# Feed-forward of a post-norm transformer layer: 32-bit operands become pairs of 16-bit halves, the psum banks go in three pairs, and work moves from VectorE to ScalarE and GpSimd

## What is computed

```python
q, k, v = x @ Wq + bq, x @ Wk + bk, x @ Wv + bv      # 16 heads of 128, q scaled by 128 ** -0.5
q, k = rotary(q), rotary(k)
attn = softmax(causal(q @ k.T)) @ v                   # per batch and head
x1 = layernorm(x + attn @ Wo + bo)                    # no gain, no offset
gate = silu((x1 @ w_gate) * s_gate)                   # weights int8, one scale for each column
up = (x1 @ w_up) * s_up
out = layernorm(x1 + ((gate * up) @ w_down) * s_down)
```

## Time and profile before

| | |
|---|---|
| median of 3 runs | 1843.8 us (1839.7 to 1846.18) |
| the profiled execution, own time | 1839.86 us |
| its span in the trace | 1838.1 us |
| PE busy | 1661.6 us, 90% of the span |
| DVE, ACT, POOL busy | 1556.7 (85%), 1397.9 (76%), 1411.7 (77%) us |
| mean granted TensorE clock | 0.993 of full speed |

### The profile page before, as it was taken

How to read it: one execution, slowest core, us unless ns; L and a number is a source line. 1 busy time by engine, 2 the same in 40 slices (tenths; PEclk the granted TensorE clock), 3 DMA queues, 4 the chain that set the end, 5 groups by cost and what they waited for, 6 DMA issues and landing times. The chain is left out here.

```text
span 1838.1 us, 34107 instructions
## 1 busy us (share of the span) xinstructions
PE 1661.6 (90%) x10508; PEld 1062.2 (58%) x10508; DVE 1556.7 (85%) x3734; ACT 1397.9 (76%) x2514; POOL 1411.7 (77%) x1331
## 2 busy tenths in 40 slices
PE   5799898898999999999999999989999999889997
PEld 3355555454555555555555555555555555468886
DVE  7799999998888888888888888888888888867886
ACT  4688778778888888888888888788888888754443
POOL 4888888788878888888888887898888887724554
PEclk9899999999999999999999999999999999999999
DMA  3666767657666676667666666676676876640001
GB/s 115 135 125 134 138 150 136 137 98 153 133 126 124 125 142 123 118 132 145 127 123 125 135 137 124 117 148 125 117 124 120 171 144 122 105 104 13 24 24 35
DMA packets 645027, 218.43 MB, mean 119 GB/s; under 512 B 610544, under 2 KB 617200, under 8 KB 644720
## 3 DMA queue, kind: packets, MB, share of 16 engines
q1 hardware_dynamic: 620784, 174.30, 50.7%
q10 hardware_dynamic: 24064, 41.95, 8.1%
HBM read 48.40 MB, written 16.78 MB: 35 GB/s over the span
## 5 line engine op out<-in xcount | busy, mean ns | idle before, releaser
L1223 DVE SCALAR_TENSOR_TENSOR planes<-S,recip,planes 128x128 f16<-128x128 f32 (+7 forms) x512 | 417.3, 815 | 130.6 <-ACT planes L883 129.9
L883 ACT ACTIVATE planes<-S,recip 128x128 f16<-128x128 f32 (+7 forms) x512 | 378.7, 740 | 155.3 <-DVE recip L1284 140.2
L874 ACT ACTIVATE S<-p_row,neg_max 128x128 f32<-128x128 f32 (+7 forms) x512 | 381.1, 744 | 131.1 <-DVE neg_max L1213 130.1
L548 POOL TENSOR_TENSOR swap<-swap,sin_t 128x512 f32<-128x512 f32 x256 | 326.3, 1275 | 169.4 <-ACT swap L896 169.4
L1213 DVE CUSTOM_DVE_ANT_0 p_row<-S,mask_row,to_score 128x128 f32<-128x128 f32 (+7 forms) x512 | 416.9, 814 | 11.1 <-PE S L1533 8.9
L542 POOL TENSOR_TENSOR rot<-rot,swap 128x512 f32<-128x512 f32 x252 | 320.1, 1270 | 68.4 <-DVE rot L1273 64.1
L896 ACT ACTIVATE swap<-S,bqx 64x512 f32<-64x512 f32 x512 | 349.6, 683 | 21.1 <-PE S L1554 8.3
L1472 PE MATMUL O<-PT,VA 128*128 128x512 f16 (+3 forms) x1152 | 216.2, 329 | 58.3 <-issue 41.8
L1472 PE MATMUL O<-PT,VB 128*128 128x512 f16 (+3 forms) x1152 | 214.7, 327 | 58.8 <-issue 41.5
L1533 PE MATMUL S<-QKA 128*128 128x512 f16 (+4 forms) x1152 | 231.7, 329 | 5.6 <-DVE planes L1223 3.5
L1533 PE MATMUL S<-QKB 128*128 128x512 f16 (+4 forms) x1152 | 229.8, 327 | 4.9 <-POOL QKB L586 2.7
(11 more groups left out here) (209 smaller groups left out, 2724.0 us busy)
## 6 DMA issues: line engine op xcount, KB each, us to landing
PT<-planes SPq DMA_TRANSPOSE x512, 3.4
WA<-w_d ACTq DMA_DIRECT2D x24, 256.0 KB, 3.7
WB<-w_d ACTq DMA_DIRECT2D x24, 256.0 KB, 2.7
attn_d<-resid ACTq DMA_DIRECT2D x16, 256.0 KB, 2.6
x_raw<-in_x_cols SPq DMA_DIRECT2D x12, 256.0 KB, 3.7
WVA<-wv_d ACTq DMA_DIRECT2D x12, 256.0 KB, 2.7
resid<-in_x_rows ACTq DMA_DIRECT2D x12, 256.0 KB, 4.0
WVB<-wv_d ACTq DMA_DIRECT2D x12, 256.0 KB, 2.7
```

The costliest lines, as they stand in the source:

```text
L548: nc.gpsimd.tensor_tensor(swap[:, c, :], swap[:, c, :], sin_t[:, half], ALU.mult).then_inc(sin_done, 1)
L874: nc.scalar.activation(row_psum(n, s)[:, 0:cols], p_row[:, k % 2, 0:cols], ACT.Exp, bias=neg_max[:, s:s + 1], scale=-1.0, accum_out=row_su ...
L883: nc.scalar.activation(row_halves(n, s)[:, 0], row_psum(n, s)[:, 0:cols].rearrange("p (j q) -> p j q", q=P), ACT.Copy, scale=recip[:, s:s ...
L1223: nc.vector.scalar_tensor_tensor(halves_of[:, 1], row_psum(n, s)[:, 0:cols].rearrange("p (j q) -> p j q", q=P), recip[:, s:s + 1], halves_ ...
```

## The change

The feed-forward matmuls get float16 operands, in high and low halves for x and fuse, and plain float16 for the int8 weights. x is scaled by 2 to the 11th (X1_UP) and the up product by a factor f_up taken from the scales, both taken out again through s_gate, s_up and s_down; these factors are made in head 58 by a few small instructions (weigh_s, sum_s, take_s, scale_s). Groups 1 to 7 use three bank pairs in turn instead of two; there are eight fuse buffers for six, and four product and Silu buffers for two each; the down product comes three steps back. The bias sums move from VectorE to GpSimd, the normalising from VectorE to ScalarE (VectorE computes `shift` = -mean * rstd for it), and the conversion of all ffn weights to GpSimd, two pieces at the end of each of heads 58, 60 and 62.

The diff, cut to its core:

```diff
-    fuse = [at(AT_QK + 4096 * i, f"fuse{i}", [P, 2, GQ], F32R) for i in range(6)]
-    ffn_w = [at(AT_X + 8192 * i, f"ffn_w{i}", [P, KT * INTER], F32R)[:, :] for i in range(2)] + [
-        at(AT_QK + 24576, "ffn_w2", [P, JT * DIM], F32R)[:, :]]
-    x1T = [[at(o, f"x1T{o}", [P, KT, GQ], F32R) for o in two] for two in ((AT_WV, AT_W), (AT_OT, AT_OT + 4096))]
+    fuse = [at(AT_QK + 16384 * (i // 4) + 2048 * (i % 4), f"fuse{i}", [P, 2, GQ]) for i in range(8)]
+    ffn_w = [at(AT_QK + o, f"ffn_w{i}", [P, KT * INTER])[:, :] for i, o in enumerate((8192, 12288, 24576))]
+    x1T = [[at(AT_OT + o + 2048 * i, f"x1T{o}{i}", [P, KT, GQ]) for i in range(2)] for o in (4096, 12288)]
...
-    fuse_f, silu = rot[:, 0:2, :], swap[:, 0:2, :]
+    fuse_f = [rot[:, 0, :], rot[:, 1, :], cos_t[:, 0:GQ], cos_t[:, GQ:]]
+    silu = [swap[:, i, :] for i in range(4)]
...
-    DOWN_AFTER = {0: [-2], 1: [-1], 2: [], 3: [0, 1], 4: [2], 5: [3], 6: [4], 7: [5]}
+    DOWN_AFTER = {0: [-3], 1: [-2], 2: [-1], 3: [], 4: [0, 1], 5: [2], 6: [3], 7: [4]}
...
+    def gate_up_psum(g, j):
+        two = [S[0][:, 0:GQ], S[0][:, GQ:]], [S[1][:, 0:GQ], S[1][:, GQ:]], [O[:, :], X[:, :]]
+        return two[j % 2 if g == 0 else (j if j <= TURN_AT else j + 1) % 3]
+
+    def last_in_banks(g, j):
+        if g == 0:
+            return j - 1
+        return 8 * g + {0: -2, 1: -1, 2: 0}.get(j, 0) + (1 if g == 1 and j < 2 else 0) if j < 3 else \
+            8 * g + {3: 1, 4: 2, 5: 4, 6: 5, 7: 3}[j]
# gpsimd
+                    if n == HEADS - 4 and s in (0, 2):
+                        pool.wait_ge(attn_in, 64)
+                        first_sum(0, s // 2)
+                    if n in (HEADS - 6, HEADS - 4, HEADS - 2) and s >= 6:
+                        ffn_weights(n - (HEADS - 6) + s - 6)
...
+                nc.gpsimd.tensor_copy(ffn_w[i][:, cols], w8[:, i, cols]).then_inc((w_ready, w_ready, wd_ready)[i], 1)
...
             def group(g, par, first, more, j):
+                if more and j == 0:
+                    first_sums(g + 1)
                 if more and j == 1:
                     inverse_root(0, g + 1)
-                if not first and j == 4:
+                if not first and j == 6:
                     inverse_root(1, g - 1)
+                pool.wait_ge(fuse_hi, 8 * g + (j + 1))
+                nc.gpsimd.tensor_tensor(fuse_of(g, j)[:, 1, :], fuse_f[j % 4],
+                                        fuse_of(g, j)[:, 0, :], ALU.subtract).then_inc(fuse_lo, 1)
# scalar
-                    if n == HEADS - 1 and s < 4:
-                        ffn_weights(s)
+                    if n == HEADS - 3 and s >= 4:
+                        if s == 4:
+                            act.wait_ge(shifted[0], 1)
+                        normal(0, 0, s - 4)
...
+                nc.scalar.activation(rows(g, t), rows(g, t), ACT.Identity, bias=shift[:, w, t:t + 1],
+                                     scale=rstd[:, w, t:t + 1]).then_inc(normalised[w], 1)
...
+                if j > 0:
+                    fuse_high(g, j - 1)
+                elif g > 0:
+                    fuse_high(g - 1, JT - 1)
+                if more and j == 3:
+                    normalise(0, g + 1)
+                if j == 0 and g > 1:
+                    normalise(1, g - 2)
# vector
-                    if n == HEADS and s == 1:
-                        ffn_down_weights()
...
-                if j == 2 and not first:
-                    down_scaled(g - 1)
+                wait(dve, fuse_lo, 8 * g + (j - 3))
...
-                if more and j == 0:
-                    first_sums(g + 1)
+                if j == 1 and not first:
+                    down_scaled(g - 1)
+                if not first and j == 4:
                     second_sums(g - 1)
-                if more and j == 3:
-                    normalise(0, g + 1)
-                if not first and j == 4:
+                if more and j == 2:
+                    shifts(0, g + 1)
+                if not first and j == 6:
                     moments(1, g - 1)
-                if not first and j == 6:
-                    normalise(1, g - 1)
+                if not first and j == 7:
+                    shifts(1, g - 1)
# tensor
+                if j == 7 and more and not first:
+                    pe.wait_ge(xt_lo, KT * (g + 1) + KT)
-                wait(pe, silued, 8 * g + (j - 1))
-                wait(pe, fused, 8 * g + (j - 1))
+                wait(pe, silued, last_in_banks(g, j))
+                wait(pe, fused, last_in_banks(g, j))
...
                 if more and j == TURN_AT and not first:
+                    pe.wait_ge(silued, 8 * g + 3)
+                    pe.wait_ge(fused, 8 * g + 3)
...
-            down(0, 5).then_inc(downed, 1)
...
-                for j in (JT - 2, JT - 1):
+                for j in (JT - 3, JT - 2, JT - 1):
```

More of the change, by code:

```diff
@@ L151, in layer @@
     rstd = sb("rstd", [P, 2, TPG])
+    shift = sb("shift", [P, 2, TPG])
     minus_half = sb("minus_half", [P, TPG])
@@ L907, in x1T_high, with normalise, normal @@
+            def normalise(w, g):
+                act.wait_ge(shifted[w], g + 1)
+                for t in range(TPG):
+                    normal(w, g, t)
+            def normal(w, g, t):
+                nc.scalar.activation(rows(g, t), rows(g, t), ACT.Identity, bias=shift[:, w, t:t + 1],
+                                     scale=rstd[:, w, t:t + 1]).then_inc(normalised[w], 1)
             def x1T_high(g, par, t):
                 act.wait_ge(xt_up, KT * g + (t + 1))
-                copy(x1T[par][0][:, t, :], turned(g, t)).then_inc(xt_hi, 1)
+                nc.scalar.activation(x1T[par][0][:, t, :], turned(g, t), ACT.Copy, scale=X1_UP).then_inc(xt_hi, 1)
@@ L912, in group @@
             def group(g, par, first, more, j):
                 act.wait_ge(gate_up, 16 * g + (2 * j + 1))
-                wait(act, fused, 8 * g + (j - 1))
-                nc.scalar.activation(silu[:, j % 2, :], S[j % 2][:, 0:GQ], ACT.Silu,
+                if first and j == 0:
+                    act.wait_ge(s_scaled, 5)
+                wait(act, fused, 8 * g + (j - 3))
+                nc.scalar.activation(silu[j % 4], gate_up_psum(g, j)[0], ACT.Silu,
                                      scale=sg_t[:, 0, j:j + 1]).then_inc(silued, 1)
-                act.wait_ge(fused, 8 * g + (j + 1))
@@ L918, in group @@
-                wait(act, downed, 8 * g + (j + 1) - len(fuse))
-                copy(fuse_of(g, j)[:, 0, :], fuse_f[:, j % 2, :]).then_inc(fuse_hi, 1)
+                if j > 0:
[6 more added lines that the diff above has]
+                    normalise(1, g - 2)
                 if more and j == TURN_AT + 1 and not first:
```

127 lines of the change are left out of this document (75 added, 52 removed).

## The result

The changed kernel takes 1826.3 us (median of 4 runs, 1824.3 to 1828.8), the kernel before 1843.6 beside it (4 runs); the ratio is 0.991, 95% interval 0.989 to 0.993. The forecast of 1828 us and its range held. Two later series on other chips gave 1826.8 and 1828.2 us, ratios 0.9905 [0.988, 0.993] and 0.9908 [0.989, 0.993]. The profiled execution took 1828.8 us, its span is 1827.0, 11.1 less than the span before. It is the slowest of its four, and the profiled one of before was near its fastest, so a single pair of profiles shows less than the medians (17 us).

What follows compares the result with a forecast made beforehand. PE was taken as the bound, a feed-forward group lasting exactly as long as its matmuls. From a median of 1843.8 us, -10.3 - 2.8 + 0.5 - 2.8 = -15.4 gave 1828 us, range 1819 to 1836.

Steps and rivals of the forecast that it cites:

- Float16 operands, -10.3 us: Feed-forward groups: float16 matmuls at 0.217 and 0.109 us shorten each of seven groups by 1.47 to 21.85 us.
- a margin of 0.5 us at the transposes: Transposes behind step 4 of a group: ScalarE normalises until 12.5 us, PE comes at 13.0, so no wait.
- The other engines keep up: In a 21.85 us group VectorE has at most 13.7 us of work, ScalarE 15.1, GpSimd 13.8; all have 6 to spare.
- Group 0, -2.8 us: Group 0: PE's 0.73 us wait goes as down-weight conversion and sums leave VectorE; shorter matmuls and a later down product add.
- The end, +0.5 us: Behind the last gate set: GpSimd's power of the second norm makes the last low part of fuse 0.5 us later.
- Heads 58 to 62, -2.8 us: Attention: 5.9 us of excess in heads 60 to 62 falls to 3.1, including GpSimd's casts and head 58's small instructions.
- Head 63, nothing: Head 63: ScalarE's conversions leave it, but it waits for the transposing DMAs, so nothing is gained.
- head 62's fall: Start of head 62: the granted clock's fall to the 1.2 GHz level, 12 matmuls taking 3.0 us, was counted as gone.
- Nothing from attention: Rival: slow casts (2.31 us) or VectorE's freed time not reaching PE leave heads without gain; 1831 to 1833 us, chance 0.17.
- GpSimd against VectorE: Rival: the two engines block each other in SBUF, costing a group up to 1.1 us; 1836 us, chance 0.13.
- The pace not from the type: Rival: the feed-forward's 0.230 us matmul pace has another source than operand type; only -4.0 left, 1840 us, chance 0.04.
- The slow cast: Rival: GpSimd's int8 cast holds up heads 59 and 61; slower from 5.1 us a cast, 1848 at 6, chance 0.03.

Runs made afterwards that it cites:

- f16_only: Kernel before with only the feed-forward operands made float16, without scale factors; ratio to before 0.9938 [0.991, 0.996], a group 22.05 us.
- norm_sums_back: Changed kernel with normalising and bias sums back on VectorE; groups 1 to 7 take 150.14 us, median 2.8 to 4.7 us above the changed kernel.
- conv_back: Changed kernel with the int8 weight conversions back on ScalarE (head 63) and VectorE (group 0), into the same float16 tiles; median 1830.4 us.
- after_third: Changed kernel run a third time, nothing edited, for a median and a third profile; heads 60 to 62 take 71.8 us.

## Why the prediction was right

*Float16 operands, -10.3 us.* Measured -11.6 for the seven groups, beyond the bound of -11 that was set: 1.64 us each instead of 1.47. The pace was 0.216 and 0.109 us as read from the earlier trace rows. Most of the rest is the transposes, which I had left at 1.0 us and which came down to 0.87: the chain of before has 0.55 and 0.44 us for them, that of the changed kernel 0.44 and 0.44. In before VectorE's normalisings end at 1723.52 and the transposes start at 1723.57, so the 0.11 may be a wait too short for the profile to list. f16_only splits the term: 9.1 us are the type, 2.5 are the waits that the shorter steps would have laid bare (0.37 a group for VectorE's normalising), and which the new order and the third pair keep away, with the moves (150.14 us) or without them (norm_sums_back, the same). The prediction counted these three at nothing and gave a margin of 0.5 us at the transposes. That held: 0.42 in the changed kernel. But the type alone, priced at 10.3, earned 9.1; that the order of before would have waits at the new pace was not seen.

*The other engines keep up.* VectorE 15.1 us in a group (13.7 forecast), ScalarE 14.4 (15.1), GpSimd 13.6 (13.8). ScalarE's normalising was 0.586 us, 24% over the row taken; VectorE's was too low since the second sums went from 0.68 to 1.11, and since this load left out the two shifts, four columns each, at 0.15 us and, beside GpSimd, 1.11. Both are hidden.

*Group 0, -2.8 us.* Measured -3.2 in the first pair of profiles, -2.6 to -3.2 over all. The wait of 0.73 is gone. conv_back and norm_sums_back corrected the reason: each of the two moves does it alone.

*The end, +0.5 us.* +0.2 to +0.3. The chain runs where it was said: moments, power, two low parts of fuse, and then PE.

```profile
1813.02 0.18 DVE var_eps L1408
1813.20 0.07 issue
1813.27 1.01 POOL rstd L679
1814.27 2.24 POOL fuse L705 x2
1816.52 0.05 issue
1816.57 0.62 PE S L1726 x4
```

*Heads 58 to 62, -2.8 us.* Measured -1.6 in the first profile, -1.3 and -2.9 in the two others. Part of this is the clock: without slow matmuls the order of before takes 122.6 us there (f16_only) and that of the changed kernel 121.2 (after_third), so the schedule gave 1.4. Of excess, 3.0 us are left where 3.1 were counted, but the parts were not right, and that they cancel is luck. Head 58 cost 1.85 us where 0.6 was counted: the seven small operations were priced by their columns, but one or two of them wait beside GpSimd, the one on 256 columns with 1.10 us (0.33 late in head 63, where GpSimd is idle) and one on 8 columns with 0.57 in two profiles, two on 8 columns with 1.13 and 0.64 in the third. Heads 60, 61 and 62 kept 0.4, 0.3 and 0.4 us of excess over the steady 23.26 and 24.24, where 1.1, 0.7 and 0.7 were counted. The casts cost nothing: 1.01 us for 1024 int8 columns instead of 1.22, and PE's wait at the start of head 60 stayed at 0.98.

*Head 63, nothing.* It is 25.5 and 27.1 us in the two profiles of before and 25.4 to 28.8 in the three of the changed kernel, so there may be nothing or about 1 us of loss, and ScalarE's freed time brought nothing. The clock, which was counted as cured with head 62's fall, does not fall there in any profile of the changed kernel, but in head 59, 61 or 63; it does so in 63 in a profile of before too. That step was wrong: a fall was taken as the cost of one place that can be removed there.

What the schedule gave, without slow matmuls, adds up to -11.6 - 3.1 + 0.3 - 1.4 = -15.8 us, and the medians give 16.6 to 17.3. The remaining 0.8 to 1.5 us fit the fall at head 62, 1.7 us, which both profiles of before have and which the changed kernel has somewhere in heads 59 to 62 in two profiles of three; more can't be said from so few. The mechanism was right, but that -15.4 and -15.8 lie so close is in part luck: the groups and group 0 gave 1.6 us more than counted, and heads 58 to 62 without the clock 1.4 less.

*The rivals.* Nothing from attention: refuted by heads 60 and 62. GpSimd against VectorE: it is there (0.68 to 1.11, 0.33 to 1.10, 0.20 to 0.84 us), but only in head 58 does it reach PE. The pace not from the type: refuted by f16_only. The slow cast: 1.01 us against 5.1.

## What to carry to other kernels

When the busiest engine's instructions become shorter, walk the other engines' chains again at the new pace: here the type alone gave 1.3 us a group and left a wait of 0.3 us that a third pair of banks with a later consumer removed, and that taking the normalising off VectorE in the old order exchanged for one of 0.24. Price a small VectorE operation by what GpSimd is doing at that moment, and not by its columns, and look at what stands behind it in the queue. Before two schedules are compared by a stage with waits in it, take several profiles of each; only stages that repeat to 0.01 us can be read from one.

## What the runs showed of the hardware

- VectorE's addition on four columns took 0.17 to 0.20 us ahead of GpSimd's cast and 0.81 to 0.84 inside it, in all profiles of the one kind and of the other.
- VectorE stood still for some 0.37 us, with no wait, ahead of the 4288th of its instructions in the trace, in seven profiles and whatever instruction stood there; in the changed kernel a product of 1.15 us stands before that place, long enough to hide it. Its cause is open.
- GpSimd casts 1024 int8 columns to float16 in 1.01 us (two in 2.02) and 512 float32 columns in 0.61; ScalarE took 1.05 for 1024 int8 columns, VectorE 1.22 for 2048 to float16 (conv_back; 1.51 in f16_only) and 1.64 to 32 bits.
- Matmuls of 32-bit operands with 512 and 256 columns go at 0.230 and 0.119 us, of float16 at 0.216 and 0.109; their weight loads take 0.189 us each with 32 bits (the 20.55 us for 138 of the earlier trace rows count overlapping ones once) and 0.098 with float16.
- A fall of the granted clock after a wait of 3.2 us came in some executions of one schedule and not in others, after 2.00 us at the start of head 59 in five of fourteen, and after waits of 1.2 and 0.7 us in one.
